# Turning three quarters of the attention output by DMA in an eight-core attention and FFN kernel

## The chip, the cores and the metric

The kernel runs on the eight cores of one Trainium2 chip. Each core runs the same program on its own two of the sixteen sequences, and no core talks to another. The metric is the device time in microseconds of the slowest core. The engines are named as the profile names them: PE (TensorE, matrix products), ACT (ScalarE), DVE (VectorE), POOL (GpSimd) and SP (SyncE). PEld is PE's weight load, which runs beside its products. In this kernel POOL and SP only issue DMAs: POOL those that convert types while loading, SP plain copies, stores and DMA transposes.

## What is computed

```python
qkv = x @ W_qkv                                  # x: (16, 2048, 1024), 16 heads of 64
# q and k rotated (rotary embedding), windows of 128 queries; a window's
# keys are its own 128 tokens and the 128 before, masked to the last 128
attn = softmax(mask(q k^T / 8)) @ v
x = layernorm(x + attn @ W_out)                  # called y below
h = silu(y @ wg^T) * (y @ wu^T)                  # hidden 3072, weights int / 127
out = layernorm(y + h @ wd^T)
```

## The kernel before, in words

A core has 4096 tokens, cut into `NT` = 8 tiles of 512. A tile `t` has four windows `w` of 128 tokens. The order of every engine's work is written out by hand, one function for each engine (`on_tensor`, `on_scalar`, `on_vector`, `on_gpsimd`, `on_sync`), and the engines meet only at counting semaphores. So an instruction that waits holds up all that stands behind it on its own engine.

The loop `for t in range(1, NT)` on PE has two stages.

**The attention stage** has eight steps `p` = 0 to 7. In step p PE runs `pv(t, p - 1)` (probabilities times values, for one half of a window's heads), `scores(t, 2p)` and `scores(t, 2p + 1)`, and `down(t - 1, p)`: 24 matmuls of 512 columns for one half row block of the previous tile's down projection. ACT takes the exponentials (`exp`), DVE masks them (`mask_p`), normalizes the result of `pv` into one half of `attn_tm` (`norm_p`, L804), adds the down projection to its residual (`res_2`) and finishes the second layernorm (`final`). Two steps make a window: after `norm_p` of step pair w, `attn_tm` (tokens on partitions) must be turned so that features lie on partitions, for use as the weights of the output projection.

In the kernel before PE turns every window. In steps 2, 4 and 6, `transp(t, w)` (L445) is eight PE transposes of 128 columns in the middle of `down`, into bank 4 of PSUM (one half of `pvb`); ACT copies them to `attn_fm` (`t_out`, L652), and after the second half of `down` comes `outp(t, w)` (L467): 2 times 8 matmuls of 512 columns, the output projection of window w, into banks 7 and 6. Window 3 follows after step 7: `pv(t, 7)`, one `qkv` block of the next tile, `transp(t, 3)`, another `qkv` block, `outp(t, 3)`. A `qkv` block is 8 matmuls of 512 columns.

`res_1` adds the input row block to the output projection, one half at a time, and takes the statistics; `rstd_1` (ACT) and `y_norm` (DVE) make y in `y_tm`. Windows 0 to 2 of y are turned by SP's DMA transposes (`turn_y`, L1124), window 3 by PE (`y_transp`) and ACT (`ty_out`). The second stage, `gate_up(t, 0)` to `gate_up(t, 23)`, needs all four; its first call waits for the semaphore `y_turn`, which the three DMA turns raise.

In the last tile (t = 7) there is no next tile, so no `qkv` blocks stand between the attention stage and `gate_up`. There PE runs `down(6, 7)` in pieces around `pv(7, 7)` and `transp(7, 3)`, then `outp(7, 3)`, then `gate_up` of windows 0 to 2 (384 columns) while window 3 is still being finished.

**SP's queue** in a tile: `store(t-1, 0)`, `turn_y(t, 0)`, `store(t-1, 1)`, `turn_y(t, 1)`, and so on, each behind its own wait, then `rotate` for the next tile (copies for the rotary embedding). **POOL's queue** at a tile's start: `xt_load` (rows of x for the residual), three weight loads for `gate_up`, then, once `scores(t, 0)` has run, another `xt_load`, `x16_load` twice (the next tile's x, 512 KB each) and three `qk_load`s (256 KB each). `xt_load(4t+2)` and `xt_load(4t+3)` wait for `res_1`. In the last tile six weight loads of 512 KB (`gx_load` 3 to 8) come one behind the other after `xt_load(4t+3)`.

PSUM has eight banks: 0 to 3 hold scores or gate and up, 4 and 5 are `pvb`, and 6 and 7 are shared by `down` (even p in 6, odd p in 7) and `outp`. `d_bank_free` and the waits in `outp` keep them apart.

Of the kernel before, what the change touches and what calls it, by code (L numbers as in the profile page):

```python
# [21 lines left out]
NT = TOK // TILE  # L22
# [36 lines left out]
O_BANK = [[7, 6], [7, 6], [7, 6], [6, 7]]  # L59
# [55 lines left out]
def build_core_program():  # L115
# [12 lines left out]
    with ExitStack() as top:  # L128
# [39 lines left out]
        def bank(b):  # L168
            if b < 4:
                return sc[:, b * 512:(b + 1) * 512]  # L170
            if b < 6:
# [5 lines left out]
                 "qk_ev", "v_ev", "exp", "t_ev", "ty_ev", "y_turn", "silu", "ln1", "rstd1", "ln2", "rstd2",  # L177
# [69 lines left out]
        q3 = q_sb.ap().rearrange("p (c n) -> p c n", c=DC)  # L247
        y3 = y_fm.ap().rearrange("p (c n) -> p c n", c=DC)
# [10 lines left out]
        ty_count = lambda t: 4 + t  # L259

# [17 lines left out]
        def on_tensor(e):  # L278
# [148 lines left out]
            def d_bank_free(t, p):  # L427
# [5 lines left out]
                if p == 2:  # L433
                    e.wait_ge(G["r2"], 8 * (t - 1) + 1)
                elif p >= 3:
                    e.wait_ge(G["r1"], 8 * t + p - 2)
# [12 lines left out]
            def outp(t, w):  # L449
                e.wait_ge(G["t_ev"], 4 * t + w + 1)  # L450
                if t == 0 and w == 0:
                    e.wait_ge(G["wo"], 16 * 8)
                for half in range(2):
# [6 lines left out]
                    elif w == 3 and half == 0:  # L460

                        e.wait_ge(G["r1"], 8 * t + 6)
                    elif t:

                        e.wait_ge(G["r2"], 8 * (t - 1) + (2 * w + 2 + half if w < 3 else 8))
                    for f in range(DC):
                        mm = e.matmul(out=bank(O_BANK[w][half]), lhsT=attn_fm[:, f * 128:(f + 1) * 128],  # L467
# [15 lines left out]
            def gate_up(t, hc, w0=0, w1=WPT):  # L483
# [3 lines left out]
                if hc == 0 or w0:  # L487
                    if t:
                        e.wait_ge(G["y_turn"], 48 * t)
# [65 lines left out]
            for t in range(1, NT + 1):  # L555
# [10 lines left out]
                for p in range(NPAIR):  # L566
                    if p:

                        if p >= 3 and p % 2 == 1:
                            e.wait_ge(G["t_ev"], 4 * t + (p - 3) // 2 + 1)  # L570
                        pv(t, p - 1)
# [7 lines left out]
                    if p % 2 == 0:  # L579
                        w = (p - 2) // 2  # L580
                        d_bank_free(t, p)
                        down(prev, p, 0, HC // 2)
                        transp(t, w)
                        down(prev, p, HC // 2, HC)
                        outp(t, w)
                    else:
                        d_bank_free(t, p)
                        if p == 7 and t == NT - 1:
                            down(prev, p, 0, 14)
                            continue  # L590
                        down(prev, p, 0, HC)
# [624 lines left out]
```

## Time and profile before

| what | value |
|---|---|
| time before, median of 3 runs | 1575.89 us (1573.59 to 1578.32) |
| the profiled execution, device time | 1580.03 us |
| span of its slowest core (core 4) | 1578.5 us |
| spans of its eight cores | 1570.6 to 1578.5 us |
| PE busy | 1528.3 us (97%) |
| PEld, DVE, ACT, POOL busy | 736.0, 623.4, 482.9, 215.1 us |
| DMA | 200.18 MB, mean 127 GB/s |

Busy time of a pipelined PE says little of its peak; what counts is which engine the chain of waits runs through. Start times are in us from the span's start. A count in a timeline can be one or two short of the code, since some matmul records are missing; the time between two starts is what to read. A chain's pieces have the length by which they moved the end, so there a group of eight transposes is 0.45 us, where the timeline shows 0.61 us from first start to last end.

### The profile page before, as it was taken

To read this page: it belongs to the slowest core of one execution; us is meant where nothing else is said; L and a number is where in the kernel's file an instruction comes from. 1 tells how busy PE (TensorE), PEld (TensorE's weight loads), DVE (VectorE), ACT (ScalarE), POOL (GpSimd) and SP (SyncE) were. 2 spreads that over 40 slices of the span, in tenths; PEclk is the share of its full clock that TensorE was granted. 3 is DMA by queue.
4 is the path that set the end of the run, shared out by engine and by line. 5 is a ranking of instruction groups with operands and counts; after the bars stand their busy time and mean duration, and the time that the engine had idled before them with its cause. 6 is when DMAs were issued, how large, how long until landed. Compare 5 with 4: busy or idle time off the path is not lost.

```text
span 1578.5 us, 24200 instructions; the slowest of 8 cores (1570.6 to 1578.5 us)
## 1 busy us (share of the span) xinstructions
PE 1528.3 (97%) x8914; PEld 736.0 (47%) x9056; DVE 623.4 (39%) x1041; ACT 482.9 (31%) x700; POOL 215.1 (14%) x398
## 2 busy tenths in 40 slices
PE   6899999999999999999999999999999999999998
PEld 2444445444454444544445444544445444455444
DVE  0763126423363323632246322562326623264223
ACT  1542234322333223432234322433224322333210
POOL 7002110011101111012110121101111011110100
PEclk9999999999999999999999999999999999999999
DMA  9998984399935989269882798737976389727911
GB/s 147 199 191 152 155 128 99 73 173 156 140 78 89 174 151 147 60 105 174 150 138 52 133 174 139 120 81 122 177 136 114 74 140 168 128 59 124 167 32 54
DMA packets 103683, 200.18 MB, mean 127 GB/s; under 512 B 33680, under 2 KB 42000, under 8 KB 103568
## 3 DMA queue, kind: packets, MB, share of 16 engines
q0 software_dynamic: 62624, 157.31, 64.7%
q1 hardware_dynamic: 40944, 41.31, 8.3%
q8 instruction: 75, 1.23, 0.3%
q14 instruction: 40, 0.33, 0.1%
HBM read 316.81 MB, written 16.78 MB: 211 GB/s over the span
## 4 chain that ended last, share of the span: by engine, by line
PE 93%; DMA 2%; DVE 2%; issue 2%; ACT 0%; another core or an unknown queue 0%; DVEq 0%; POOL 0%; ACTq 0%; POOLq 0%; SPq 0%
PE sc L510 41%; PE dn L410 20%; PE dn L467 6%; PE dn L323 6%; PE pvb L323 5%; PE dn L330 3%; PE pvb L330 2%; PE sc L371 2%; PE pvb L390 2%; PE sc L323 2%; DMA gu<-wgu_d 1%; PE pvb L445 1%; DMA wv<-wv_d 1%; PE sc L330 1%; DMA y_fm<-y_tm 1%
## 5 line engine op out<-in xcount | busy, mean ns | idle before, releaser
L510 PE MATMUL sc<-y_fm,gu 128*128 128x512 bf16 (+1 forms) x2583 | 579.6, 377 | 7.8 <-DMA y_fm<-y_tm 2.0
L510 PEld LDWEIGHTS sc<-y_fm,gu 128*128 128x128 bf16 x2656 | 259.0, 98 | 313.5 <-issue 6.7
L880 DVE TENSOR_TENSOR h_sb<-pt,sc 128x512 bf16<-128x512 bf16 x190 | 130.6, 688 | 624.6 <-PE sc L510 572.7
L410 PE MATMUL dn<-wd,h_sb 128*128 128x512 bf16 x1453 | 331.5, 379 | 7.1 <-issue 6.0
L682 ACT ACTIVATE pt<-sc,consts 128x512 bf16<-128x512 f32 x190 | 130.4, 687 | 322.2 <-PE sc L510 322.1
L410 PEld LDWEIGHTS dn<-wd,h_sb 128*128 128x128 bf16 x1512 | 141.7, 98 | 164.7
L647 ACT ACTIVATE pt<-sc,consts 128x1024 f16<-128x1024 f32 x112 | 129.6, 1199 | 217.1 <-PE sc L371 217.0
L1020 POOL DMA_DIRECT2D gu<-wgu_d x165 | 87.3, 529 | 625.5 <-PE sc L510 585.3
L467 PE MATMUL dn<-wo,attn_fm 128*128 128x512 f16 x512 | 117.4, 383 | 2.8 <-DMA wo<-wo_d 2.1
L841 DVE SCALAR_TENSOR_TENSOR r<-dn,consts,y_tm 128x512 f32<-128x512 f32 x62 | 46.6, 751 | 120.4 <-PE dn L410 120.4
L1007 POOL DMA_DIRECT2D qk<-wqk_d x96 | 53.4, 562 | 258.8 <-PE sc L323 179.2
L787 DVE TENSOR_TENSOR pt<-pt,mask 128x1024 f16<-128x1024 f16 x112 | 73.4, 686 | 21.2 <-ACT pt L647 21.2
L467 PEld LDWEIGHTS dn<-wo,attn_fm 128*128 128x128 f16 x512 | 50.3, 99 | 65.2 <-issue 6.6
L323 PE MATMUL pvb<-x,qk 128*128 128x512 f16 x336 | 79.4, 379 | 0.0
L323 PE MATMUL dn<-x,qk 128*128 128x512 f16 x288 | 68.0, 379 | 0.0
L631 ACT CAST qraw<-pvb 128x512 f16<-128x512 f32 x47 | 27.6, 588 | 113.0 <-PE pvb L323 109.6
L631 ACT CAST qraw<-dn 128x512 f16<-128x512 f32 x46 | 26.9, 585 | 111.4 <-PE dn L323 111.4
L776 DVE TENSOR_TENSOR rotb<-rotb,cs 128x1024 f16<-128x1024 f16 x56 | 38.5, 688 | 40.5 <-DMA rotb<-qraw 40.3
L323 PEld LDWEIGHTS pvb<-x,qk 128*128 128x128 f16 x336 | 32.8, 98 | 39.7
L1001 POOL DMA_DIRECT2D xt<-x_tm x30 | 16.2, 548 | 247.8 <-DVE r L820 247.4
L820 DVE TENSOR_TENSOR r<-dn,xt 128x512 f16<-128x512 f32 x60 | 41.5, 691 | 19.5 <-PE dn L467 19.5
L823 DVE BATCH_NORM_STATS2 st<-r 128x6 f32<-128x512 f16 x64 | 44.4, 694 | 6.6
(164 smaller groups left out, 1199.3 us busy)
## 6 DMA issues: line engine op xcount, KB each, us to landing
gu<-wgu_d POOLq DMA_DIRECT2D x165, 512.0 KB, 7.6
qk<-wqk_d POOLq DMA_DIRECT2D x96, 256.0 KB, 8.0
out_tm<-r SPq DMA_DIRECT2D x31, 512.0 KB, 2.6
rotb<-qraw SPq DMA_DIRECT2D x224, 64.0 KB, 5.9
xt<-x_tm POOLq DMA_DIRECT2D x30, 256.0 KB, 7.1
x<-x_fm POOLq DMA_DIRECT2D x14, 512.0 KB, 14.5
wd<-wgu_d POOLq DMA_DIRECT2D x12, 512.0 KB, 72.7
wd<-wd_d POOLq DMA_DIRECT2D x24, 256.0 KB, 10.9
```

The lines of the kernel that those rows point to most:

```text
L323: mm = e.matmul(out=dst, lhsT=wt[:, dc * 128:(dc + 1) * 128], rhs=x_of(t, dc), start=(dc == 0), stop=(dc == DC - 1))
L330: mm = e.matmul(out=dst, lhsT=x_of(t, dc)[:, w * 128:(w + 1) * 128], rhs=wv[:, dc * 1024 + half * 512:dc * 1024 + (half + 1) * 512], start ...
L410: mm = e.matmul(out=bank(D_BANK[p]), lhsT=h_sb[:, hc * TILE + w * 128:hc * TILE + (w + 1) * 128], rhs=wd[:, hc * 1024 + half * 512:hc * 10 ...
L467: mm = e.matmul(out=bank(O_BANK[w][half]), lhsT=attn_fm[:, f * 128:(f + 1) * 128], rhs=wo[:, f * 1024 + half * 512:f * 1024 + (half + 1) * ...
L510: mm = e.matmul(out=bank(b0 + part)[:, w0 * 128:w1 * 128], lhsT=wt[:, part * 1024 + dc * 128:part * 1024 + (dc + 1) * 128], rhs=y_fm[:, dc ...
L631: e.copy(out=raw_of(t, j)[:, (i % 2) * 512:(i % 2 + 1) * 512], in_=src).then_inc(G["qk_ev"], 1)
L647: e.activation(out=pt_of(t, u), in_=sc[:, sb0:sb0 + 1024], func=AF.Exp, bias=consts[:, 0:1], scale=consts[:, 5:6]).then_inc(G["exp"], 1)
L682: e.activation(out=a_sb[hc % 2], in_=bank(gu_bank(t, hc)), func=AF.Silu, scale=consts[:, 1:2]).then_inc(G["silu"], 1)
L787: e.tensor_tensor(out=p3, in0=p3, in1=maskb, op=ALU.min).then_inc(G["mask"], 1)
L880: e.tensor_tensor(out=h_sb[:, hc * TILE:(hc + 1) * TILE], in0=a_sb[hc % 2], in1=bank(gu_bank(t, hc) + 1), op=ALU.mult).then_inc(G["h"], 1)
L1007: e.dma_start(out=qk[n % 3][:], in_=wqk_d[i]).then_inc(qk_ld[n % 3], 16)
L1020: e.dma_start(out=gu[r % 3][:], in_=wgu_d[n % HC]).then_inc(gu_ld[r % 3], 16)
```

## The change

For tiles 1 to 7 windows 0 to 2 of `attn_tm` are no longer turned by PE and copied by ACT. SP issues a DMA transpose for each half (`turn_attn`), straight from `attn_tm` to `attn_fm`; it waits for that half's `norm_p`, and from window 1 on for the previous window's `outp`, which still reads `attn_fm`. `norm_p` now waits, before it overwrites a half of `attn_tm`, until that half's last turn has landed. Tile 0, and window 3 of each tile, stay as they were.

`outp(t, w)` of windows 0 to 2 moves from the end of step 2w + 2 to the end of step 2w + 3, and with it `res_1`, `rstd_1` and `y_norm` on DVE and ACT; `outp` uses banks 6 and 7 in this order. Those of window 2 now come after step 7: `res_1(t, 2, 1)`, `rstd_1(t, 2)` behind `t_out(t, 3)` on ACT, and `y_norm(t, 2)`. SP's queue is written out anew: turns of attention, stores and turns of y interleaved, with `turn_y(t, 2)` last ahead of the `rotate`s. In the last tile `outp(7, 2)` is put after the first 8 chunks of `down(6, 7)`, into banks 0 and 1; `gate_up` also waits for `res_1` of window 2; and POOL issues `gx_load` 3 to 5 at the tile's start and 6, 7 and 8 one by one, each after a window's second half has been turned. Leading blanks are shortened in the diff.

```diff
@@ -56,7 +56,16 @@
-O_BANK = [[7, 6], [7, 6], [7, 6], [6, 7]]
+def o_bank(t, w, half):
+    if w < 3 and t == 0:
+return 7 - half
+    if w == 2 and t == NT - 1:
+return half
+    return 6 + half
@@ -174,7 +183,7 @@
-    "qk_ev", "v_ev", "exp", "t_ev", "ty_ev", "y_turn", "silu", "ln1", "rstd1", "ln2", "rstd2",
+    "qk_ev", "v_ev", "exp", "t_ev", "ty_ev", "y_turn", "at_turn0", "at_turn1", "silu", "ln1", "rstd1", "ln2", "rstd2",
@@ -245,6 +254,7 @@
+afm3 = attn_fm.ap().rearrange("p (c n) -> p c n", c=DC)
@@ -257,6 +267,7 @@
 ty_count = lambda t: 4 + t
+t_count = ty_count
@@ -430,10 +441,10 @@
       if p >= 2:
         e.wait_ge(G["r2"], 8 * (t - 1) + p - 1)
       return
-    if p == 2:
-      e.wait_ge(G["r2"], 8 * (t - 1) + 1)
-    elif p >= 3:
-      e.wait_ge(G["r1"], 8 * t + p - 2)
+    if p == 2 or p == 3:
+      e.wait_ge(G["r2"], 8 * (t - 1) + p - 1)
+    elif p >= 4:
+      e.wait_ge(G["r1"], 8 * t + p - 3)
   def transp(t, w):
     e.wait_ge(G["nrm"], 8 * t + 2 * w + 2 if t else 7 + w // 2)
@@ -447,9 +458,15 @@
     mm.then_inc(G["t_mm"], 1)
   def outp(t, w):
-    e.wait_ge(G["t_ev"], 4 * t + w + 1)
-    if t == 0 and w == 0:
-      e.wait_ge(G["wo"], 16 * 8)
+    if t == 0:
+      e.wait_ge(G["t_ev"], w + 1)
+      if w == 0:
+        e.wait_ge(G["wo"], 16 * 8)
+    elif w == 3:
+      e.wait_ge(G["t_ev"], t_count(t))
+    else:
+      e.wait_ge(G["at_turn0"], 16 * (3 * (t - 1) + w + 1))
+      e.wait_ge(G["at_turn1"], 16 * (3 * (t - 1) + w + 1))
     for half in range(2):
       if t == 0:
@@ -457,14 +474,20 @@
           e.wait_ge(G["qk_ev"], 20 - half)
         else:
           e.wait_ge(G["r1"], 2 * w - 1 + half if w < 3 else 6 - half)
-      elif w == 3 and half == 0:
-        e.wait_ge(G["r1"], 8 * t + 6)
-      elif t:
-        e.wait_ge(G["r2"], 8 * (t - 1) + (2 * w + 2 + half if w < 3 else 8))
+      elif w == 3 and t == NT - 1:
+        e.wait_ge(G["r2"], 8 * t - 1 + half)
+      elif w == 3:
+        e.wait_ge(G["r1"], 8 * t + 5 + half)
+      elif w == 2 and t == NT - 1:
+        e.wait_ge(G["exp"], 16 * t + 15)
+      else:
+        e.wait_ge(G["r2"], 8 * (t - 1) + 2 * w + 3 + half)
       for f in range(DC):
-        mm = e.matmul(out=bank(O_BANK[w][half]), lhsT=attn_fm[:, f * 128:(f + 1) * 128],
+        mm = e.matmul(out=bank(o_bank(t, w, half)), lhsT=attn_fm[:, f * 128:(f + 1) * 128],
                rhs=wo[:, f * 1024 + half * 512:f * 1024 + (half + 1) * 512],
                start=(f == 0), stop=(f == DC - 1))
       mm.then_inc(G["o_mm"], 1)
@@ -485,6 +508,9 @@
     n = 24 * t + hc
     b0 = gu_bank(t, hc)
     if hc == 0 or w0:
+      if t == NT - 1:
+        e.wait_ge(G["r1"], 8 * t + 6)
       if t:
         e.wait_ge(G["y_turn"], 48 * t)
       if w1 == WPT:
@@ -565,9 +591,6 @@
     e.wait_ge(G["rope"], 8 * (t + 1))
     for p in range(NPAIR):
       if p:
-        if p >= 3 and p % 2 == 1:
-          e.wait_ge(G["t_ev"], 4 * t + (p - 3) // 2 + 1)
         pv(t, p - 1)
       scores(t, 2 * p)
       if p == 0:
@@ -576,25 +599,21 @@
         down(prev, 0, HC // 2, HC)
         continue
       scores(t, 2 * p + 1)
-      if p % 2 == 0:
-        w = (p - 2) // 2
+      if p == 7 and t == NT - 1:
         d_bank_free(t, p)
-        down(prev, p, 0, HC // 2)
-        transp(t, w)
-        down(prev, p, HC // 2, HC)
-        outp(t, w)
-      else:
-        d_bank_free(t, p)
-        if p == 7 and t == NT - 1:
-          down(prev, p, 0, 14)
-          continue
-        down(prev, p, 0, HC)
+        down(prev, p, 0, 8)
+        outp(t, 2)
+        continue
+      d_bank_free(t, p)
+      down(prev, p, 0, HC)
+      if p >= 3 and p % 2 == 1:
+        outp(t, (p - 3) // 2)
     pv(t, 7)
     if t == NT - 1:
-      down(prev, 7, 14, 19)
+      down(prev, 7, 8, 15)
       transp(t, 3)
-      down(prev, 7, 19, HC)
+      down(prev, 7, 15, HC)
       outp(t, 3)
       gate_up(t, 0, 0, 3)
       gate_up(t, 1, 0, 3)
@@ -648,7 +667,7 @@
             bias=consts[:, 0:1], scale=consts[:, 5:6]).then_inc(G["exp"], 1)
   def t_out(t, w):
-    e.wait_ge(G["t_mm"], 4 * t + w + 1)
+    e.wait_ge(G["t_mm"], w + 1 if t == 0 else t_count(t))
     e.copy(out=attn_fm[:], in_=tr16 if t else tr16_0[w % 2]).then_inc(G["t_ev"], 1)
   def ty_out(t, w):
@@ -725,15 +744,14 @@
       exp(t, 2 * p)
       exp(t, 2 * p + 1)
       if p % 2 == 0 and p >= 2:
-        if t:
-          rstd_2(t - 1, (p - 2) // 2)
-        t_out(t, (p - 2) // 2)
-      elif p >= 3:
-        rstd_1(t, (p - 3) // 2)
+        rstd_2(t - 1, (p - 2) // 2)
+      if p % 2 == 0 and p >= 4:
+        rstd_1(t, (p - 4) // 2)
     if nxt:
       rstd_2(t - 1, 3)
       qkv_out(t + 1, ORDER[0])
     t_out(t, 3)
+    rstd_1(t, 2)
     if nxt:
       qkv_out(t + 1, ORDER[1])
       qkv_out(t + 1, ORDER[2])
@@ -792,6 +810,9 @@
     e.reciprocal(out=recb.ap().unsqueeze(2), in_=pv3[:, :, 64:65]).then_inc(G["rec"], 1)
     e.wait_ge(G["rec"], n + 1)
     half = p % 2
+    if t and p >= 2:
+      e.wait_ge(G[f"at_turn{half}"], 16 * (3 * (t - 1) + p // 2))
     if t == 0:
       g = p // 2
       e.tensor_tensor(out=attn0_w[:, 2 * half:2 * half + 2, 256 * g:256 * g + 256].rearrange(
@@ -813,11 +834,11 @@
       e.wait_ge(xt_ld[n % 2], 16 * max(1, n // 2))
     xw = xt0[n - 2] if n in (2, 3) else xt[n % 2]
     hs = slice(half * 512, (half + 1) * 512)
-    if t == 0 and w and half == 0:
+    if n and half == 0:
       e.wait_ge(G["y"], n)
     e.wait_ge(G["o_mm"], 2 * n + half + 1)
-    e.tensor_tensor(out=r1[:, hs], in0=bank(O_BANK[w][half]), in1=xw[:, hs],
+    e.tensor_tensor(out=r1[:, hs], in0=bank(o_bank(t, w, half)), in1=xw[:, hs],
             op=ALU.add).then_inc(G["r1"], 1)
     e.wait_ge(G["r1"], 2 * n + half + 1)
     e.bn_stats(out=st1[:, 6 * half:6 * half + 6], in_=r1[:, hs]).then_inc(G["bn1"], 1)
@@ -941,25 +962,28 @@
   for t in range(1, NT):
     nxt = t + 1 < NT
     for p in range(NPAIR):
-      if p >= 3 and p % 2 == 1:
-        res_1(t, (p - 3) // 2, 1)
+      if p % 2 == 0 and p >= 4:
+        res_1(t, (p - 4) // 2, 1)
       if p:
         norm_p(t, p - 1)
       mask_p(t, 2 * p)
       mask_p(t, 2 * p + 1)
       if p == 4 and (t + 1) % TPS:
         carry()
-      if p % 2 == 0 and p >= 2 and t:
+      if p % 2 == 0 and p >= 2:
         final(t - 1, (p - 2) // 2)
-      if p >= 3 and p % 2 == 1:
-        y_norm(t, (p - 3) // 2)
+      if p % 2 == 0 and p >= 4:
+        y_norm(t, (p - 4) // 2)
       if nxt or p < 7:
         res_2(t - 1, p)
-      if p % 2 == 0 and p >= 2:
-        res_1(t, (p - 2) // 2, 0)
+      if p % 2 == 1 and p >= 3:
+        res_1(t, (p - 3) // 2, 0)
     norm_p(t, 7)
+    res_1(t, 2, 1)
     if nxt:
       final(t - 1, 3)
+    y_norm(t, 2)
+    if nxt:
       rope_cos(t + 1, 0)
     else:
       res_2(t - 1, 7)
@@ -1072,6 +1096,27 @@
     for i in range(3):
       gu_load(24 * t + i)
     e.wait_ge(G["s_mm"], 16 * t + 1)
+    if not nxt:
+      e.wait_ge(G["qk_mm"], 16 * NT)
+      e.wait_ge(G["v_mm"], 8 * NT)
+      for i in range(3):
+        gx_load(3 + i)
+      xt_load(4 * t + 1)
+      e.wait_ge(G["at_turn1"], 16 * (3 * (t - 1) + 1))
+      gx_load(6)
+      xt_load(4 * t + 2)
+      e.wait_ge(G["at_turn1"], 16 * (3 * (t - 1) + 2))
+      gx_load(7)
+      xt_load(4 * t + 3)
+      e.wait_ge(G["at_turn1"], 16 * (3 * (t - 1) + 3))
+      gx_load(8)
+      for hc in range(9, HC):
+        if in_gx(t, hc):
+          gx_load(hc)
+        else:
+          gu_load(24 * t + hc)
+      break
     xt_load(4 * t + 1)
     if nxt:
       x16_load(t + 1, 0)
@@ -1083,19 +1128,9 @@
     if nxt:
       for i in range(3, 6):
         qk_load(t + 1, i)
-    else:
-      e.wait_ge(G["qk_mm"], 16 * NT)
-      e.wait_ge(G["v_mm"], 8 * NT)
-      for i in range(6):
-        gx_load(3 + i)
-      for hc in range(9, HC):
-        if in_gx(t, hc):
-          gx_load(hc)
-        else:
-          gu_load(24 * t + hc)
-    for hc in range(HC - 3 if nxt else 0):
+    for hc in range(HC - 3):
       gu_load(24 * t + hc + 3)
-      if SLOT.get(hc, NQKV) + 3 < 16:
+      if nxt and SLOT.get(hc, NQKV) + 3 < 16:
         qk_load(t + 1, SLOT[hc] + 3)
@@ -1118,6 +1153,13 @@
     s, a, b = rows_of(t, w)
     e.wait_ge(G["fin"], n + 1)
     e.dma_start(out=out_tm[s, a:b, :], in_=r2[n % 2][:]).then_inc(out_st[n % 2], 16)
+  def turn_attn(t, w, half):
+    e.wait_ge(G["nrm"], 8 * t + 2 * w + half + 1)
+    if w and half == 0:
+      e.wait_ge(G["o_mm"], 8 * t + 2 * w)
+    e.dma_start(out=afm3[:, 4 * half:4 * half + 4, :], in_=attn_tm[:, half * 512:(half + 1) * 512],
+          transpose=True).then_inc(G[f"at_turn{half}"], 16)
   def turn_y(t, w):
     e.wait_ge(G["y"], 4 * t + w + 1)
@@ -1136,10 +1178,22 @@
     if nxt:
       tab_load(t + 1)
     if t:
-      for w in range(WPT):
-        store(t - 1, w)
-        if w < 3:
-          turn_y(t, w)
+      turn_attn(t, 0, 0)
+      turn_attn(t, 0, 1)
+      store(t - 1, 0)
+      turn_attn(t, 1, 0)
+      turn_attn(t, 1, 1)
+      store(t - 1, 1)
+      turn_y(t, 0)
+      turn_attn(t, 2, 0)
+      turn_attn(t, 2, 1)
+      store(t - 1, 2)
+      turn_y(t, 1)
+      if nxt:
+        store(t - 1, 3)
+      turn_y(t, 2)
+      if not nxt:
+        store(t - 1, 3)
     if nxt:
       for j in range(8):
         rotate(t + 1, j)
```

## Rows read from the trace of the kernel before

**Rows 1.** Spans of the cores: us, mean granted clock
```profile
core 3: 1575.9 us, clock 0.997
...
core 4: 1578.5 us, clock 0.996
```

**Rows 2.** Page, the chain that ended last by engine
```profile
PE 93%; DMA 2%; DVE 2%; issue 2%; ACT 0%; another core or an unknown queue 0%; DVEq 0%; POOL 0%; ACTq 0%; POOLq 0%; SPq 0%
```

**Rows 3.** PE's waits, core 4: line, releaser: us in total, times, longest
```profile
PE pvb L445 <- DVE attn_tm L804: 4.9, 7, 0.8
...
PE sc L510 <- DMA y_fm<-y_tm: 2.0, 1, 2.0
...
PE dn L467 <- ACT attn_fm L652: 0.3, 1, 0.3
```

**Rows 4.** The same view, core 3, last tile
```profile
PE sc L510 <- DMA y_fm<-y_tm: 0.6, 1, 0.6
```

**Rows 5.** Chain of waits, tile 2: start us, us, what
```profile
432.30 0.45 PE pvb L445 x8
...
435.34 3.45 PE dn L467 x16
...
445.12 0.49 PE pvb L390 x16
...
478.33 0.76 DVE r L841
...
479.19 0.71 DVE st L845
...
480.39 0.70 DVE attn_tm L804
...
481.23 0.61 PE pvb L445 x8
```

**Rows 6.** Timeline, tile 2: start us, us, engine, line, operation, count
```profile
418.09 1.49 POOL L987 DMA_DIRECT2D x<-x_fm  x2 [0.28 <-issue]
...
419.57 1.63 POOL L1007 DMA_DIRECT2D qk<-wqk_d  x3
...
424.10 0.69 DVE L804 TENSOR_TENSOR attn_tm<-pvb,recb 128x512 f16<-128x512 f32 x1
...
430.73 0.69 DVE L804 TENSOR_TENSOR attn_tm<-pvb,recb 128x512 f16<-128x512 f32 x1
```

**Rows 7.** Stretches, tile 2: PE, PEld, DVE, ACT, POOL busy, PEclk, DMA share, GB/s
```profile
436.00:437.00 1.00, 1.00 (x6) 0.49 (x5) 0.89 (x2) 0.00 (x0) 0.00 (x0) 1.00 1.02 320
...
438.00:439.00 1.00, 1.00 (x17) 0.65 (x16) 0.76 (x2) 0.00 (x0) 0.00 (x0) 1.00 0.07 27
```

**Rows 8.** SP's turns of y_tm: issue in the last tile, landing of all
```profile
1419.74 1.35 SPq L1124 DMA_TRANSPOSE y_fm<-y_tm  x1
...
DMA to landing us min/median/max: 3.0/3.1/23.3
```

**Rows 9.** Chain of waits, last tile
```profile
1436.29 8.87 DMA y_fm<-y_tm
...
1445.41 7.04 PE sc L510 x32
...
1452.89 2.60 PE dn L510 x16
```

**Rows 10.** Timeline, last tile
```profile
1438.51 1.01 ACT L652 COPY attn_fm<-pvb 128x1024 f16<-128x1024 f16 x1 [2.98 <-PE pvb L445]
...
1445.78 0.29 ACT L665 ACTIVATE rs<-rs,consts 128x1 f32<-128x1 f32 x1
...
1446.18 0.55 DVE L831 TENSOR_SCALAR y_tm<-r,ag,rs 128x1024 bf16<-128x1024 f16 x1 [0.88 <-ACT rs L665]
```

**Rows 11.** The same view: a stretch with a pause of PE, one after a pause
```profile
480.00:482.00 2.00, 1.21 (x13) 0.67 (x11) 1.78 (x4) 1.13 (x4) 0.91 (x1) 1.00 0.00 0
...
1447.00:1449.00 2.00, 2.00 (x8) 0.91 (x7) 0.00 (x0) 0.00 (x0) 0.00 (x0) 0.50 0.00 0
```

## Prediction

> **What bounds the kernel now.** I read four views in this order. The spans of the cores show that all eight are within 8 us and at full clock, and that no core stands out [rows 1]. The chain that ended last runs through PE for 93% of the span [rows 2]: only what shortens PE's own work, or a wait of PE, shortens the kernel. ACT, DVE, POOL and SP matter only where PE waits for them. PE's waits give those places [rows 3]: 4.9 us in seven pieces, all ahead of the transposes of window 3 and released by `norm_p`; 2.0 us once, ahead of the last tile's first `gate_up`, released by a DMA turn of y; 0.3 us for ACT's copy. The reader should see that windows 0 to 2 have no wait worth naming now: the change must earn there by removing PE's work, and it must not put a wait in its place. The chain of tile 2 gives the price of that work: eight transposes move the end by 0.45 us, an `outp` by 3.45 us [rows 5]. The timelines and the DMA rows then tell when a turn by DMA can land.
>
> **Part 1: PE's transposes removed.** Tiles 1 to 7, three windows each: 21 groups at 0.45 us [rows 5] = 9.45 us, all on the chain. The matmuls of `down` around them are the same; a lower bound of nothing has no reason in the rows, since the piece is one of the chain itself. ACT loses 21 copies of 1.01 us [rows 10], which is worth nothing, since PE is not waiting for them except the 0.3 us, below.
>
> Here a rule of the notes can be weighed against the row. Eight transposes in 0.45 us are 56 ns each. The Trainium skill, page "VectorE: DVE Perf Modes", section "The three transpose paths", gives 390 ns for a 128x128 transpose on TensorE and 1309 ns for one by DMA, and in "Rules for kernel authors" prefers TensorE where PSUM will do. By its 390 ns the 168 removed transposes would give back an estimated 66 us; by the row it is 9.45 us, and I keep the row.
>
> **Part 2: the pause before window 3's transposes.** Before, DVE ran `res_2(t-1, 7)` (0.76 and 0.71 us) between the end of `down` and `norm_p(7)`, so PE, with only `pv` and one `qkv` block to do, waited 0.8 us [rows 3, 5]. After, `outp(t, 2)` stands between `down` and `pv(7)`. Count from the end of `down`: PE reaches the transposes after 3.45 + 0.49 + 1.73 (half an `outp`, the size of a `qkv` block) = 5.67 us. DVE does `res_2` in the first 1.7 us, the first half of `res_1` (two operations of that size) from 1.9 to 3.4 us, and then waits for `pv`, which ends at 3.94; the reciprocal, L804 (0.70) and the release take at most 1.33 us (from the end of L845 at 479.90 to the transposes at 481.23) [rows 5]. That is 5.27, or 0.4 us early. So all of it goes in six tiles, and in the last, where the wait was 0.2 us, 0.1 us of margin is left (below). Gain 4.9 us; if the cover fails, the gain is between 0 and 4.9.
>
> **Part 3: the last tile.** Before, the last turn of y took 8.87 us from issue to landing beside six `gx_load`s; PE waited 2.0 us [rows 3, 9] and then ran at the 1.2 GHz level for about two microseconds [rows 11], so 32 matmuls of 384 columns took 7.04 us, where 16 of them at full clock took 2.60 [rows 9]: 1.84 us lost. After, `y_norm(7, 2)` comes later, behind `t_out(7, 3)` and `rstd_1`. Count from the end of `outp(7, 2)`. `pv` 0.49 and 7 matmuls of 0.216 bring PE to the transposes at 2.00 (L804 can be done at 0.49 + 1.33 = 1.82). They end at 2.45; ACT's copy (0.2 later, 1.01) at 3.7; `rstd_1` (two of 0.29) at 4.4; `y_norm` (0.55) at 5.05 [rows 10]. The turn, 3.1 us when nothing else moves [rows 8], lands at 8.25 and releases PE at 8.5 (the release took 0.25 before: 1445.16 to 1445.41 [rows 9]). PE, with 9 more matmuls and `outp(7, 3)`, is there at 7.84. New wait: 0.65 us. A pause of 0.8 us left the clock at full [rows 11], so I count no loss of clock. `res_2(6, 7)` stands behind `y_norm` on DVE and ends at 5.85; the second half of `outp(7, 3)`, which needs it, starts at 6.12. On core 4 this part gives -2.0 - 1.84 - 0.3 + 0.65 = -3.5 us. On core 3, which waited only 0.6 us [rows 4], it gives -0.3.
>
> **Part 4: the turns by DMA, and what waits for them.** A whole turn of 1024 columns takes 3.0 to 3.1 us in quiet and took up to 23.3 us beside loads [rows 8]. A half turn is not in the trace; in quiet I bound it by 1.5 and 3.1 us. Windows 1 and 2 are easy: their turns are issued at the latest when the previous `outp` ends, a step pair (16 us) less 3.45 us before their own `outp`, and in tiles 1 to 6 POOL loads next to nothing then. `norm_p`, `mask_p` behind it on DVE and `pv` behind that on PE have a step's margin. `turn_y` and the stores stand behind them on SP and have room too: `gate_up` comes some 20 us after step 7, and the `rotate`s behind `turn_y(t, 2)` are needed only by DVE before `gate_up`'s first product.
>
> Window 0 is the tight one. In tile 2 the loads for the next tile start at 418.09 and 419.57, and the halves are ready at 424.8 and 431.4 [rows 6], in the midst of them. The DMA engines stay full until the loads are done: share 1.02 at 436 to 437, 0.07 at 438 to 439 [rows 7]. `outp(2, 0)` moves from 435.34 to the end of step 3, which was at 445.12 and now comes 0.45 + 3.45 us earlier: 441.2 [rows 5]. So the second half has 9.8 us. Early end: it lands with the loads at 438.4, 2.8 us early. Late end: it starts in earnest only when they are done, and they are stretched by it: 438.4 + 3.1 + 3.1 = 444.6, 3.4 us late. The nearest row is the last tile's turn of 1419.74, which landed at 1443.04, and the next one, issued at 1436.29 and landed at 1445.16 [rows 8, 9]: once the loads let go, a whole turn was through in 2.1 us. With 2.1 us of extra work for two halves, and the store now queued behind them, I get about 440.5, in time by 0.7 us. In the last tile, three `gx_load`s take the place of the six other loads; I allow 0.5 us of wait there. I take 0 us for tiles 1 to 6, and 0 to 3.4 us a tile for the range.
>
> **The sum.** Core 4: 1578.5 - 9.45 - 4.9 - 3.5 + 0.5 = 1561.2 us. Core 3: 1575.9 - 9.45 - 4.9 - 0.3 + 0.5 = 1561.8 us, now the slowest. With the 1.5 us between span and device time, the profiled execution of 1580.03 would become 1563.3, or 16.7 us less. The profiled one is 4.1 us above the median of the runs; part of its pause on core 4 may be its own, so I take 15.4 us off the median: **1560.5 us**.
>
> **The rivals.**
> A, the turns of window 0 come a little late, by about 1 us in each of seven tiles, because loads and turns share the DMA engines. For it: 23.3 us beside loads. Against: here the loads end 3 us before the need. 1560.5 + 7 = 1567.5 us.
> B, the other side: they come late enough to slow the clock too. The place is `outp(t, 0)`; the price is a wait of 2.0 us and 1.84 us of lost clock, as in the last tile before, times seven: +27 us, 1587 us. It decides from 15.4 / 7 = 2.2 us a tile, clock included; below that the change still gains. For it: the late end of Part 4. Against: the 2.1 us of the last turn.
> C, the last turn of y is slow again. Were it 8.87 us as before, PE would wait 5.8 us more and lose the clock: +7.6 us, 1568 us. Against it: `gx_load` 8 should be over by then. By the skill's 1309 ns a block (same page and section) eight blocks would take an estimated 10.5 us, and this would happen even in quiet; the 3.1 us of the trace speaks against that.
> D, DVE doesn't reach `norm_p(7)` in time, and the 4.9 us stay: 1565.4 us.
> E, turns disturb loads and rotations elsewhere, or the device time doesn't follow PE's work: within 0.3% of before. The change can hardly fail to do what it says: the transposes are gone from PE's list.
>
> **How the numbers follow.** Forecast (waits under 1 us in sum) 0.60; A 0.16; B 0.07; C 0.07; D 0.07; E 0.03. A measurement of this kernel can tell about 0.3% from no change, 4.7 us: faster ends at 1571.2. The forecast, D, nearly all of C and most of A lie below: 0.86; part of A and C, and E, make 0.07; B and a rest 0.07. The range of the forecast alone is 1556 to 1565. Cut to leave out B, E and the far end of A, it is 1556 to 1573. The low end is the median less 9.45 + 4.9 + 4.15 us (all that core 4 could lose, with no new wait), less 1.5 us for the spread of runs; the high end is A with almost 2 us a tile.
>
> **What would show each step.** Right: L445 in the pvb group falls from 224 to 56 matmuls; PE's wait for L804 falls from 4.9 to under 0.5 us; the chain piece of 0.45 us is gone from steps 2, 4, 6; a wait of L467 for DMA attn_fm<-attn_tm is absent or under 1 us a tile; the last `gate_up` waits 0.3 to 1.0 us and PEclk stays 1.00 behind it. Wrong: L467 waiting seven times for the turn, above all with PEclk under 1.00 after it (A, B); a landing of the last turn over 5 us (C); the pause before L445 still there (D). A wait of `scores` or `pv` for a mask would mean that `norm_p` itself was held by the turn, which I take to have a step's margin.

## The result, and the profile after

| | before | changed |
|---|---|---|
| median of the timed runs | 1575.34 us (4 runs, 1573.59 to 1578.32) | 1559.25 us (4 runs, 1557.91 to 1562.47) |
| profiled execution, device time | 1580.03 us | 1557.91 us |
| spans of the cores | 1570.6 to 1578.5 us | 1551.8 to 1556.4 us |

The ratio is 0.9896, with a 95% interval of 0.9883 to 0.9908: faster by 16.1 us. Three later timings of the same kernel beside that of before gave 0.9896 (0.9883 to 0.9909), 0.9896 (0.9881 to 0.9912) and 0.9892 (0.9875 to 0.991). Every ratio leaves out executions in which some cores ran at a clearly lower granted clock and the whole took longer; the trace of e9 below is of such a one and is read on core 5, whose clock was 0.997.

The page of the changed kernel: PE's busy time (with PE's share and count, then the other engines), and the chain by engine.

```profile
PE 1526.3 (98%) x8888; PEld 726.0 (47%) x8888; DVE 624.0 (40%) x1041; ACT 462.4 (30%) x679; POOL 213.5 (14%) x398
...
PE 95%; DMA 2%; DVE 1%; ACT 1%; issue 1%; POOL 0%; SPq 0%; DVEq 0%; ACTq 0%; POOLq 0%
```

PE's share of the chain went from 93 [rows 2] to 95%. PE's waits on the slowest core, core 6 (line, releaser: total, times, longest):

```profile
PE dn L490 <- DVE r L841: 0.4, 1, 0.4
...
PE sc L536 <- DMA y_fm<-y_tm: 0.3, 1, 0.3
```

Set this beside [rows 3]. The seven waits for `norm_p` (4.9 us) are gone. The first `gate_up` of the last tile waits 0.3 us instead of 2.0, and no `outp` of this core waits for a turn: on core 4 one wait of 0.2 us is all that any core shows. The 0.4 us line is of tile 0, which the change doesn't touch.

The chain of tile 2 (start, us, what), beside [rows 5]:

```profile
435.93 3.45 PE dn L490 x16
...
452.04 3.45 PE dn L490 x16
...
468.14 3.45 PE dn L490 x16
471.60 0.49 PE pvb L401 x16
472.08 1.73 PE sc L334 x8
473.81 0.45 PE pvb L456 x8
```

No PE transposes stand between the three `outp`s any more. They are 16.1 us apart, where a pair of steps took 16.55 before (`pv` starts at 445.12 [rows 5] and, one pair later, at 461.67). At the tile's end `pv` and one `qkv` block lead straight into window 3's transposes, and these count 0.45 us, not the 0.61 of 481.23 [rows 5].

The best ruler turned out to be the start of each tile's first `scores`. For tiles 1 and 7 it is, in the timeline of the kernel before (core 4):

```profile
223.96 0.40 PE L371 MATMUL sc<-q_sb,k_sb 64*128 64x128 f16 x8
```

```profile
1375.96 0.40 PE L371 MATMUL sc<-q_sb,k_sb 64*128 64x128 f16 x8
```

and in that of the changed kernel (core 6):

```profile
220.98 0.40 PE L382 MATMUL sc<-q_sb,k_sb 64*128 64x128 f16 x8
```

```profile
1359.19 0.40 PE L382 MATMUL sc<-q_sb,k_sb 64*128 64x128 f16 x8
```

So six tiles took 1152.0 us before and 1138.2 after: 13.8 us less, 2.30 us a tile. From there to the end of the span it was 1578.5 - 1376.0 = 202.5 us on core 4 and is 1556.4 - 1359.2 = 197.2 us. On core 5, which had no wait in the last tile, it was 1573.8 - 1375.0 = 198.8 us. That makes 15.4 us for a core like core 5 and 19.1 us for one like core 4; the timed 16.1 us lies between. The changed kernel's core 6 is 3.0 us ahead at the start of tile 1 already, where the order of work is still the same in both. The eight cores start tile 1 at 219.9 to 224.1 us in the profile of before, at 216.3 to 221.0 in that of the changed kernel, and at 218.4 to 224.4 in e2 below. In another profile of the changed kernel itself (e11) it is 218.0 to 224.6. So it is scatter of the start, and I leave it out of the change's account. Part of it are PE's waits for the first loads in tile 0: core 4 before waited 2.1 us for `wo` and 2.0 us for `gu`, core 6 of the changed kernel for neither.

### The profile page after: what moved, and what is told of

Same layout as the page of the kernel before. It is cut to its first block, busy times and chain, and to the rows that moved or that the text cites. A ratio compares the mean times of both kernels' runs of the same rounds, so it can differ in the third digit from the quotient of the medians.

```text
span 1556.4 us, 24118 instructions; the slowest of 8 cores (1551.8 to 1556.4 us)
## 1 busy us (share of the span) xinstructions
PE 1526.3 (98%) x8888; PEld 726.0 (47%) x8888; DVE 624.0 (40%) x1041; ACT 462.4 (30%) x679; POOL 213.5 (14%) x398
## 4 chain that ended last, share of the span: by engine, by line
PE 95%; DMA 2%; DVE 1%; ACT 1%; issue 1%; POOL 0%; SPq 0%; DVEq 0%; ACTq 0%; POOLq 0%
PE sc L536 42%; PE dn L421 21%; PE dn L490 6%; PE dn L334 5%; PE pvb L334 5%; PE dn L341 3%; PE pvb L341 2%; PE sc L334 2%; PE sc L382 2%; PE pvb L401 2%; DMA wv<-wv_d 1%; PE sc L341 1%; DMA rotb<-qraw 0%; ACT wd L666 0%; PE pvb L501 0%
## 5 line engine op out<-in xcount | busy, mean ns | idle before, releaser
L536 PE MATMUL sc<-y_fm,gu 128*128 128x512 bf16 (+1 forms) x2656 | 585.8, 376 | 0.3 <-DMA y_fm<-y_tm 0.3
L421 PE MATMUL dn<-wd,h_sb 128*128 128x512 bf16 x1512 | 337.7, 379 | 0.0
L490 PE MATMUL dn<-wo,attn_fm 128*128 128x512 f16 x496 | 112.1, 379 | 0.4 <-DVE r L841 0.4
L866 DVE BATCH_NORM_STATS2 st<-r 128x6 f32<-128x512 f32 x62 | 43.0, 694 | 6.4
```

Source lines behind the costliest of these rows:

```text
L421: mm = e.matmul(out=bank(D_BANK[p]), lhsT=h_sb[:, hc * TILE + w * 128:hc * TILE + (w + 1) * 128], rhs=wd[:, hc * 1024 + half * 512:hc * 10 ...
L490: mm = e.matmul(out=bank(o_bank(t, w, half)), lhsT=attn_fm[:, f * 128:(f + 1) * 128], rhs=wo[:, f * 1024 + half * 512:f * 1024 + (half + 1 ...
L536: mm = e.matmul(out=bank(b0 + part)[:, w0 * 128:w1 * 128], lhsT=wt[:, part * 1024 + dc * 128:part * 1024 + (dc + 1) * 128], rhs=y_fm[:, dc ...
```

## The experiments

Each kernel is the changed one with the edit shown, unless it says otherwise. The kernel before ran beside each on the same chip.

**e1, the changed kernel again.**

> The changed kernel once more, as the yardstick for the kernels beside it. Expected: 16 us under the kernel before (ratio 0.990), as in its first timing; PE's wait ahead of the last tile's first gate_up 0.3 to 0.4 us; no wait of outp for a turn over 0.3 us.

Measured: 1559.27 us against 1575.6, ratio 0.9896 (0.9883 to 0.9909). The last `gate_up` waits 0.3 us, as expected. One `outp` of the slowest core waits 0.4 us for a turn, and one each of cores 0 and 6 waits 0.8 us: a little over the 0.3 us that I had allowed.

**e2, the new order with PE's turns.** `transp`, `t_out` and their semaphore waits are back for windows 0 to 2, and SP's `turn_attn`s are out.

```diff
-                    down(prev, p, 0, HC)
+                    if p % 2 == 0 and p >= 2:
+                        down(prev, p, 0, HC // 2)
+                        transp(t, (p - 2) // 2)
+                        down(prev, p, HC // 2, HC)
+                    else:
+                        down(prev, p, 0, HC)
```

> The changed order of work (outp one step later, window 2 after step 7, last tile's loads spread), but windows 0 to 2 turned by PE and copied by ACT as before. My account: PE's 21 groups of transposes are back, so it is 9.45 us slower than the changed kernel and about 7 us faster than the kernel before (4.9 us of the pause ahead of window 3's transposes, the rest from the last tile). Rival 1, the DMA turns are what bought everything, the order alone nothing: equal to the kernel before, with the 0.8 us pauses back. Rival 2, the transposes were hidden in PE's pipeline and cost the chain less than 0.45 us a group: within 4 us of the changed kernel.

Measured: ratio to before 0.9981 (0.9946 to 1.0016), median 1569.92 us. The interval is wide because two of the nine executions behind it took 1587.44 and 1588.71 us; the other seven took 1566.93 to 1570.8, with 1567.99 in their middle, 7.6 us under before and 8.7 over e1. The profile answers more exactly. The starts of `scores` of tiles 2 and 3 (core 1):

```profile
415.56 0.40 PE L382 MATMUL sc<-q_sb,k_sb 64*128 64x128 f16 x8
```

```profile
606.75 0.40 PE L382 MATMUL sc<-q_sb,k_sb 64*128 64x128 f16 x8
```

A tile is 191.19 us long: 0.96 less than before (192.16) and 1.34 more than changed (189.85). So the order alone buys 0.96 us a tile, and the DMA turns 1.34 = 3 times 0.45 us. No core of e2 waits ahead of window 3's transposes any more. The median spans of the dies say the same: 1565.8 and 1564.6 us, against 1555.6 and 1554.5 with DMA turns, some 10 us apart. In the last tile too the pauses are gone: from its start to the end it takes 198.6 us on core 0, the turns of three windows (1.35 us) more than changed. e2 has the new order and the held loads together, so it doesn't tell which of the two took the last tile's pauses away. Rival 1 (the order buys nothing) and rival 2 (the transposes cost less) both fall.

**e3, the last tile's loads as before.** The new branch of POOL is out and the old one is back: six `gx_load`s behind `xt_load(4t+3)`.

```diff
-                    for i in range(3):
-                        gx_load(3 + i)
...
-                    e.wait_ge(G["at_turn1"], 16 * (3 * (t - 1) + 3))
-                    gx_load(8)
+                    for i in range(6):
+                        gx_load(3 + i)
```

> The changed kernel with the last tile's six gx_loads issued one behind the other after xt_load of window 3, as before. My account: turns of the last tile then move beside 3 MB of loads. The second half of window 2, ready at the start of step 6, lands some 10 to 20 us late, outp(7, 2) waits for it, the last turn of y stands behind, and the clock falls: 8 to 25 us slower than the changed kernel. Rival, the held loads are of no use because the turns get through (packets of both interleave): within 2 us of it.

Measured: 1574.67 us, ratio 0.9994 (0.9985 to 1.0003), about 15 us slower than e1: the whole gain is gone. PE's waits (core 3), and three stretches of two microseconds (PE, PEld, DVE, ACT, POOL busy, PEclk, DMA share, GB/s):

```profile
PE sc L490 <- DMA attn_fm<-attn_tm: 14.1, 1, 14.1
```

```profile
1416.00:1418.00 2.00, 0.00 (x0) 0.00 (x0) 0.00 (x0) 0.00 (x0) 0.00 (x0) 1.00 0.96 137
1418.00:1420.00 2.00, 0.00 (x0) 0.00 (x0) 0.00 (x0) 0.00 (x0) 0.00 (x0) 0.52 1.13 192
...
1428.00:1430.00 2.00, 2.00 (x6) 0.68 (x5) 0.00 (x0) 0.00 (x0) 0.00 (x0) 0.50 1.10 248
```

`outp(7, 2)` waits 14.1 us for its turn, in which the DMA engines are full. `outp(7, 2)` starts at 1426.96, so the pause began at 1412.9. The granted clock stands at 1.2 GHz from about 1418 on, 5 us into the pause, and stays there through the `outp` that follows. The rival (turns get through beside loads) falls. The hold is a needed part of the change.

**e4, window 3 by DMA too.** In tiles 1 to 6 `transp(t, 3)` and `t_out(t, 3)` go, `outp(t, 3)` stands behind three `qkv` blocks, `y_transp(t, 3)` behind three more.

```diff
-                qkv(t + 1, ORDER[0])
-                transp(t, 3)
-                qkv(t + 1, ORDER[1])
+                for k in range(3):
+                    qkv(t + 1, ORDER[k])
                 outp(t, 3)
-                for k in range(2, 5):
+                for k in range(3, 6):
                     qkv(t + 1, ORDER[k])
                 y_transp(t, 3)
```

> The changed kernel with window 3 of tiles 1 to 6 turned by DMA too; outp(t, 3) stands one qkv block later and y_transp(t, 3) one block later. My account: 6 groups of 0.45 us leave PE: 2.7 us faster than the changed kernel, if the turn of the second half (ready about 1.3 us after pv 7) lands within the 3.9 us that the blocks give it. Rival: beside the qk loads it takes 5 to 8 us, PE waits 1 to 4 us in each of six tiles, and it is 3 to 20 us slower than the changed kernel.

Measured: 1562.25 us, ratio 0.9911 (0.9896 to 0.9925): no gain over e1, if anything 3 us worse. But it isn't the expected place that waits. PE's waits (core 6), then the DMAs issued from 471 to 476 us (tensor, queue, count, KB, us to landing):

```profile
PE sc L536 <- DMA y_fm<-y_tm: 5.5, 6, 1.9
...
PE dn L490 <- DMA attn_fm<-attn_tm: 0.3, 1, 0.3
```

```profile
qk<-wqk_d POOLq DMA_DIRECT2D x2, 256.0 KB, 6.8
out_tm<-r SPq DMA_DIRECT2D x1, 512.0 KB, 5.1
attn_fm<-attn_tm SPq DMA_TRANSPOSE x2, 2.4
y_fm<-y_tm SPq DMA_TRANSPOSE x1, 11.7
```

The turns of attention land in 2.4 us, and `outp` is in time. The turn of y for window 2, issued last at 475.98, beside two `qk` loads and a store, took 11.7 us. On core 6 `gate_up` waited for it at the end of five of the tiles 1 to 6, 5.2 us in sum (the sixth wait in the line is the last tile's 0.3 us, which the changed kernel has too); on the other cores these waits come to between nothing (cores 0 and 1) and 5.2 us (core 7). Both of my alternatives missed this; e9 follows it up.

**e5, DMA turns at the old place.** The kernel before, with `turn_attn` for windows 0 to 2 and the last tile's loads held, but `outp` left in steps 2, 4 and 6. SP's queue starts with window 0's two turns, as in the changed kernel; for windows 1 and 2 a `turn_y` stands between the halves.

```diff
-                        down(prev, p, 0, HC // 2)
-                        transp(t, w)
-                        down(prev, p, HC // 2, HC)
+                        down(prev, p, 0, HC)
                         outp(t, w)
```

> The kernel before with windows 0 to 2 turned by DMA, but outp left at the end of the same step, and the last tile's loads spread as in the change. My account: the second half of window 0 is ready 4 us before outp and lands with the end of the tile's loads, so PE waits about 4.4 us there in each of seven tiles and loses about 1.8 us to the clock after each; windows 1 and 2 are in time. 1575 - 9.5 - 3.5 + 43 = 1605 us. Rival, the clock doesn't fall: 1593 us. Rival, outp could have stayed where it was: 1562 us, and the step's delay was not needed.

Measured: 1602.59 us against 1580.83, ratio 1.0137 (1.0101 to 1.0172): 22 us slower than before. PE's waits (core 0), and `outp(2, 0)` in the timeline:

```profile
PE dn L472 <- DMA attn_fm<-attn_tm: 18.3, 6, 4.1
...
PE pvb L446 <- DVE attn_tm L806: 5.8, 7, 1.2
```

```profile
440.55 5.30 PE L472 MATMUL dn<-wo,attn_fm 128*128 128x512 f16 x16 [2.83 <-DMA attn_fm<-attn_tm]
445.69 0.65 PE L391 MATMUL pvb<-vhat,pt 128*128 128x65 f16 x16
```

Six waits of 3.05 us on the mean for the turn of window 0, in tiles 1 to 6, where I expected seven of 4.4. After such a wait the 16 matmuls take until 445.69 = 5.14 us instead of 3.45: the 1.7 us of lost clock. And the pauses of `norm_p` stay, 5.8 us. On core 0 the clock fell after all six. So the gain hangs on moving `outp` a step later, and the mechanism of rival B is shown at its place: with the old order DMA turns lose 22 us.

**e6 and e7, one and three idle turns.** They stand in SP's queue ahead of window 0's second half and turn part of `wo` into buffers that are free then (waits on ACT and SP keep those buffers from being used too early). They measure the room.

```diff
                     turn_attn(t, 0, 0)
+                    idle_turns(t)    # 1 or 3 transposes of 128 x 1024
                     turn_attn(t, 0, 1)
```

> The changed kernel with one idle DMA transpose of 128 x 1024 (from wo into rotb, used by nobody) in SP's queue ahead of window 0's second half, tiles 1 to 7. It measures how near the place is to a wait. My account: it lands 2.1 us later, of 2.4 us to spare: 0 to 3 us slower than the changed kernel. Rival, beside the loads a whole turn takes 8 us and more: a wait of about 6 us a tile and the clock lost, 50 us slower.

> The same with three idle turns (into rotb 0 and 1 and qraw 1). My account: it lands 6.3 us later, PE waits 3.9 us in each of seven tiles and loses 1.8 us to the clock after each: 40 us slower than the changed kernel. Rival, the clock stays up: 27 us slower. Rival, the room is larger than I read from the trace: less than 10 us slower.

Measured: e6 ratio 0.9887 (0.9858 to 0.9915), from two executions (1561.46 and 1562.4 us), no different from the changed kernel, and no `outp` waits more than 0.2 us for a turn on any core. e7 0.9935 (0.9913 to 0.9957), 1569.35 us: about 7.6 us slower by the difference of the ratios (0.9935 - 0.9887 of 1580.8), not 40. PE's waits in e7 (core 5), then two of the `outp`s behind such a wait:

```profile
PE dn L490 <- DMA attn_fm<-attn_tm: 4.3, 3, 2.2
...
PE dn L490 <- DVE r L864: 1.0, 1, 1.0
```

```profile
822.52 5.30 PE L490 MATMUL dn<-wo,attn_fm 128*128 128x512 f16 x16 [2.25 <-DMA attn_fm<-attn_tm]
```

```profile
1015.56 3.61 PE L490 MATMUL dn<-wo,attn_fm 128*128 128x512 f16 x16 [1.34 <-DMA attn_fm<-attn_tm]
```

After 1.34 us of waiting the `outp` still takes 3.61 us; after 2.25 us it takes 5.30. In tile 2 the second half landed at 440.9 us (issued 438.40, landed 2.5 us later), 25.5 us after the tile's first `scores` (415.36). In the changed kernel it was 434.9 - 411.7 = 23.2 us (e1), so three idle turns moved it by 2.3 us, 0.8 us each. Over tiles 1 to 6 of all cores the medians agree: 25.0 us in e7, 22.4 to 23.2 in the four profiles of the changed kernel. I had put 2.1 us on each. The rest of an idle turn goes through beside the loads, before their end. The line of 1.0 us names L864, which is `res_2`, but it was the turn again. That wait is in tile 1: DVE's `norm_p` isn't held there, and its `res_2` at 249.55 is the fourth of the tile, while the first half of `outp(1, 0)` needs only the third. The second half of the turn, though, was issued at 247.72 and landed 2.5 us later, at 250.2, and PE went on 0.24 us after that:

```profile
247.72 1.19 SPq L1165 DMA_TRANSPOSE attn_fm<-attn_tm  x1
```

```profile
attn_fm<-attn_tm SPq DMA_TRANSPOSE x1, 2.5
```

```profile
250.44 3.61 PE L490 MATMUL dn<-wo,attn_fm 128*128 128x512 f16 x16 [1.00 <-DVE r L864]
```

So core 5 waited four times for a turn, 5.3 us in all.

**e8, e9 and e10, the `qk` loads held.** e8 is the changed kernel, e9 is e4 with the edit below, e10 the changed kernel with the same edit.

> The changed kernel again, as the yardstick for the two beside it: ratio 0.990 to the kernel before.

```diff
                 if nxt:
+                    e.wait_ge(G["y_turn"], 48 * t)
                     for i in range(3, 6):
                         qk_load(t + 1, i)
```

> The kernel of e4 (window 3 of tiles 1 to 6 by DMA too), with POOL holding the next tile's qk loads 3 to 5 until the three turns of y have landed. In e4 PE waited 5.5 us in six pieces ahead of gate_up for turn_y(t, 2), which took 11.7 us beside those loads. My account: with the loads held that turn takes 3 to 5 us, the six waits go, and what stays is the 2.7 us of the six groups of transposes: 2.7 us faster than the changed kernel, ratio about 0.988 to the kernel before. Rival, the held loads come late for the first qkv blocks among gate_up: PE waits for qk and it is 2 to 15 us slower than the changed kernel. Rival, the turn is slow because of the store and the rotations on its own queue: the six waits stay, and it is no faster than e4.

> The changed kernel with that hold alone (window 3 by PE). Both my account and the second rival of e9: no more than 1 us from the changed kernel, since gate_up doesn't wait for turn_y(t, 2) there. The first rival of e9: slower by the same 2 to 15 us as e9.

Measured: e8 1560.7 us, 0.9896 (0.9881 to 0.9912); e9 0.9885 (0.9866 to 0.9903), from two executions (1558.43 and 1559.9 us); e10 1562.72 us, 0.9902 (0.9888 to 0.9916). In e9 the turn of y for window 2 in tile 2 (core 5; line of the DMAs issued from 466 to 480 us) is quick:

```profile
y_fm<-y_tm SPq DMA_TRANSPOSE x1, 3.9
```

The waits of e4 in tiles 1 to 6 are gone on every core, so the loads were their cause, and not the queue of SP. Nothing waits for `qk`. On three cores `outp(t, 3)` now and then waits for its own turn, at the longest 1.6 us (core 5, tile 2). e10 shows that the hold alone buys nothing. In e8 the slowest core shows a wait of 0.9 us ahead of an `outp`; the line names `res_2`, but the turn landed 0.24 us before PE went on, as in e7.

**e11 and e12, once more with the changed kernel beside it.**

> The changed kernel, beside e12 on one chip: ratio 0.990 to the kernel before.

> The kernel of e9 once more, since its interval and that of the changed kernel overlapped there. My account: 2.7 us under the changed kernel (ratio 0.988 against 0.990). Rival: the 2.7 us are spent on small waits elsewhere, so the difference is under 1 us.

Measured: e11 1561.82 us, 0.9892 (0.9875 to 0.991); e12 1560.41 us, 0.9888 (0.9871 to 0.9906). The starts of tiles 1 and 7 in e12 (core 5):

```profile
221.00 0.40 PE L382 MATMUL sc<-q_sb,k_sb 64*128 64x128 f16 x8
```

```profile
1356.54 0.40 PE L382 MATMUL sc<-q_sb,k_sb 64*128 64x128 f16 x8
```

Six tiles take 1135.5 us, 2.7 us less than in the changed kernel: in the trace the expected gain is there in full. In the timed runs it came out at 1.4 us, inside the intervals, so that e12 beats the changed kernel is not shown by time. Of the missing 1.3 us, 0.4 go in the last tile, which takes 197.6 us from its first `scores` to the end in e12 and 197.2 in the changed kernel; the rest is within the scatter of the start (the slowest core of e12's profile starts tile 1 at 224.9 us, 3.9 later than core 5).

## Why the prediction was right, point by point

**The time.** 1560.5 us was forecast and 1559.25 measured, inside 1556 to 1573. Of the cases it was the forecast one: PE's waits for turns of window 0 sum to nothing on core 6, and in the four profiles of the changed kernel (the first, e1, e8, e11) the longest on any core is 0.9 us.

**Part 1, PE's transposes.** 9.45 us was expected. Measured by e2 against the changed kernel: 1.34 us a tile, 0.45 a group, as the chain's piece said. The estimate of 66 us by the Trainium skill's 390 ns (page "VectorE: DVE Perf Modes", section "The three transpose paths") doesn't hold for this kernel: turns in the middle of other matmuls cost 1.34 us for 24 blocks, 56 ns a block.

**Part 2, the pause.** It went in all seven tiles. The term was a little small: a pause of 0.80 us counted 0.96 us in the tile's length (e2), because the transposes behind it moved the chain by 0.61 us and not 0.45 [rows 5]. Rival D is out.

**Part 3, the last tile.** A wait of 0.65 us was forecast and 0.3 came, with the clock at full behind it. The count of times holds: `y_norm(7, 2)` and the first `gate_up` in the timeline of the changed kernel, and the turn between them in the list of DMAs (the last number is us to landing):

```profile
1420.76 0.55 DVE L852 TENSOR_SCALAR y_tm<-r,ag,rs 128x1024 bf16<-128x1024 f16 x1 [0.89 <-ACT rs L684]
...
1424.65 5.36 PE L536 MATMUL sc<-y_fm,gu 128*128 128x384 bf16 x32 [0.31 <-DMA y_fm<-y_tm]
```

```profile
y_fm<-y_tm SPq DMA_TRANSPOSE x1, 3.0
```

The end of `outp(7, 2)`, where `pv(7, 7)` starts, is 1416.34. From there `y_norm` starts after 4.4 us (forecast 4.5) and `gate_up` after 8.3 us (forecast 8.5). Its 32 matmuls take 5.36 us in place of 7.04 [rows 9]. The last tile became 5.3 us shorter on a core like core 4 (1.35 of it the transposes) and 1.6 us on one like core 5. e3 shows the condition: without the held loads the last tile alone eats the gain. Rival C is out as long as the hold is there. By the 1309 ns for a block of the Trainium skill (page "VectorE: DVE Perf Modes", section "The three transpose paths") the turn of eight would have taken an estimated 10.5 us; it took 3.0.

**Part 4, the turns of window 0.** This was the open term, and its outcome was right with some luck in the size. SP's timeline of tile 2 in the changed kernel (core 6; two issues merged), the landing of the second half, and two stretches (columns as in [rows 7]):

```profile
419.59 7.82 SPq L1161 DMA_TRANSPOSE attn_fm<-attn_tm  x2
428.14 0.34 SPq L1155 DMA_DIRECT2D out_tm<-r  x1
```

```profile
attn_fm<-attn_tm SPq DMA_TRANSPOSE x1, 7.3
```

```profile
433.00:434.00 1.00, 1.00 (x6) 0.45 (x5) 1.00 (x3) 0.00 (x0) 0.00 (x0) 1.00 1.02 415
434.00:435.00 1.00, 1.00 (x6) 0.49 (x5) 0.67 (x2) 0.00 (x0) 0.00 (x0) 1.00 0.04 12
```

The second issue takes 1.2 of the 7.8 us, so it starts at about 426.2; it lands 7.3 us later, at 433.5; `outp` starts at 435.93. So 2.4 us were to spare here and not 0.7. The room isn't steady: over tiles 1 to 6 of all cores in the four profiles of the changed kernel it is 0.2 us (which is a turn that PE waited for, or nearly) to 5.2 us, with medians of 1.7 to 2.5. The mis-sized term is the work that two halves add: I took 2.1 us after the end of the loads, as for the whole turn of the last tile [rows 8, 9], but the second half landed at 433.5 with the loads still running. e7 gives 0.8 us for a whole turn that has had time beside the loads. The first half took 13.1 us from issue to landing, so rival A's reason was real, but it had nobody waiting on PE.

**What a step's margin was worth.** I expected `norm_p` to have a step's margin. It hadn't: in the changed kernel DVE waited five times for the first half's turn ahead of L825:

```profile
  DMA attn_fm<-attn_tm: 5.5, 5
```

That cost PE nothing, since DVE had the time. In e8 one such wait lasted 1.97 us (core 1, tile 4), and the `res_2` behind it still started as soon as its `down` had ended. The mechanism was named and its margin was wrong, without a price in any profile here.

**Rival B** was rightly unlikely here and is what happens one step to the side (e5): a late turn costs its wait, and on core 0 of e5 1.7 us of clock with it.

**The sum.** On core 4 the forecast was 1578.5 - 1561.2 = 17.3 us (the 16.7 is for the slowest core, which was to be core 3); the parts that the change made there are 13.8 + 5.3 = 19.1. The gap of 1.8 is 6 times 0.16 for the pauses' true size, 0.5 for the wait that I had allowed in the last tile and that did not come, and 0.35 for the shorter wait of `gate_up`. Taking 15.4 us off the median was a choice between the sums for core 3 (14.1) and core 4 (17.3). It is what core 5's parts measured, but that the time came out within 1.3 us of the forecast is partly luck: the cores differ by more than that in the last tile and in their start.

## What to carry to other kernels

A transpose on the busiest engine costs only its slot in the stream (0.45 us for eight blocks here), and handing it to DMA pays only where the consumer stands far enough behind the producer: here 4 us of distance lost 22 us, while 10 us of distance gained 16, of which the turns by DMA made some 9.4 (e2) and the new order with the held loads the rest. Look for the loads that will be in flight when the turn is issued, because these set its landing (2.4 to 13.1 us for the same transfer), and hold them or move the consumer before moving the transpose. A short pause ahead of a group of transposes can be worth nearly as much as the transposes (0.96 against 1.34 us a tile here): fill it with work that has to be done anyway.

## What the runs showed of the hardware that I had not expected

- An idle DMA transpose of 128 x 1024 ahead in the queue, issued while the loads fill the DMA engines, delayed what stood behind it by only 0.8 us (e7), although such a turn beside loads took up to 23.3 us to land [rows 8] (and 12.7 us on the median in e6).
- PE waited 1.34 us without its clock falling and 2.25 us with the clock at 1.2 GHz afterwards (e7); before, it waited 2.0 us and the clock fell too [rows 3, 11]. In 14.1 us of waiting the clock fell after about 5 us (e3). But the length of the wait alone doesn't decide. On core 4 of e5 the `outp` behind a wait of 1.97 us takes 5.30 us at the lower clock, and the one behind 3.60 us of waiting takes 3.61 us, with the granted clock at 1.00 throughout:

```profile
242.26 5.30 PE L472 MATMUL dn<-wo,attn_fm 128*128 128x512 f16 x16 [1.97 <-DMA attn_fm<-attn_tm]
```

```profile
1213.83 3.61 PE L472 MATMUL dn<-wo,attn_fm 128*128 128x512 f16 x16 [3.60 <-DMA attn_fm<-attn_tm]
```

  What the fall costs is the slower work behind the pause: 1.7 us for an `outp`.
- The eight cores of one profile start tile 1 within 4.2 us of each other before, 4.6 us in the changed kernel and 6.6 us in e11, though they run the same program. This scatter is a quarter to two fifths of the gain, and it bears on which core is the slowest; differences of 1 to 3 us between kernels are better read from tile to tile in one trace than from medians.
